# A graph kernel's edge loop: ScalarE takes over the region ends, and the order of its fillers, loads and lower parts is laid out anew

## The reference, cut to what matters

```
x  : 1024 x 512, 16384 edges (src, dst, weight), sorted by dst
A  = zeros(1024, 1024).at[src, dst].add(weight);  deg = sum(A, axis=1)
An = dinv[:, None] * A * dinv[None, :]
h  = x;  for l in 0, 1:  h = leaky_relu((An @ h @ W_gcn[l] + b_gcn[l]) @ W_mlp[l] + b_mlp[l])
x1 = layernorm(x + h)
C  = count of the edges src -> dst, plus self loops;  dis = 1/sqrt(column sums)
h  = relu(dis * C^T (dis * x1 @ W1) + b1);  y = dis * C^T (dis * h @ W2) + b2
out = layernorm(x1 + y)
```

## Time and profile before

| | us |
|---|---|
| median of 3 runs (363.58 to 365.18) | 363.71 |
| the profiled execution | 362.79 |
| its span, first to last instruction | 361.0 |
| TensorE busy | 327.1 (91%) |
| VectorE busy | 191.9 (53%) |
| ScalarE busy | 105.8 (29%) |

### The profile page before, as it was taken

The page is one execution under the profiler, slowest core; times in us unless marked ns, Lnnn a source line. Parts: engine busy times, 40 slices in busy tenths (PEclk is TensorE's granted clock), DMA queues, the critical chain, the costliest instruction groups (busy, mean ns, idle before and its releaser), DMA issues.

```text
span 361.0 us, 5012 instructions
## 1 busy us (share of the span) xinstructions
PE 327.1 (91%) x1976; PEld 266.1 (74%) x1976; DVE 191.9 (53%) x358; ACT 105.8 (29%) x183; POOL 49.4 (14%) x54
## 2 busy tenths in 40 slices
PE   2777998788949989999999999999999999999993
PEld 1555777466737878888888888888888888888882
DVE  6994676963142446103655326767690354323655
ACT  2151336242342344101344201313550355220000
POOL 2000000000010059601000001122184000000111
PEclk9998999999987999999999999999999999999998
DMA  6121003060000000000015000000700000000212
GB/s 228 27 63 58 0 7 114 3 232 4 0 3 0 0 2 0 2 0 0 2 36 196 2 0 0 3 0 2 249 17 0 0 2 0 0 4 3 87 61 87
DMA packets 8592, 13.45 MB, mean 37 GB/s; under 512 B 1906, under 2 KB 2290, under 8 KB 8564
## 3 DMA queue, kind: packets, MB, share of 16 engines
q1 hardware_dynamic: 8564, 13.05, 10.7%
HBM read 10.95 MB, written 2.10 MB: 36 GB/s over the span
## 4 chain that ended last, share of the span: by engine, by line
PE 82%; DVE 12%; issue 3%; ACT 1%; DMA 1%; DVEq 0%; POOLq 0%; POOL 0%; SPq 0%; ACTq 0%
PE psum L568 71%; PE psum L613 5%; DVE hot L912 2%; PE psum L554 2%; PE psum L601 2%; DVE wm_low L984 1%; DVE hot L909 1%; DVE wgt_low L971 1%; DVE sel L907 1%; PE psum L731 1%; DVE adj L966 1%; DMA src_i<-in_src 1%; PE psum L654 1%; PE psum L765 0%; ACT adj L403 0%
## 5 line engine op out<-in xcount | busy, mean ns | idle before, releaser
L613 PEld LDWEIGHTS psum<-hot,sel 128*128 128x128 bf16 x512 | 30.9, 103 | 17.0 <-issue 12.6
L613 PE MATMUL psum<-hot,sel 128*128 128x96 bf16 x512 | 35.6, 218 | 6.2 <-DVE hot L912 3.1
L389 POOL TENSOR_TENSOR small<-small 128x1 f32<-128x1 f32 x16 | 11.9, 742 | 162.4 <-DVE small L1135 162.4
L568 PE MATMUL psum<-at_high,x_high 128*128 128x512 f32 x64 | 26.5, 415 | 1.7 <-DVE x_low L1063 1.7
L568 PE MATMUL psum<-at_high,x_low 128*128 128x512 f32 x64 | 25.6, 401 | 0.0
L568 PE MATMUL psum<-at_low,x_high 128*128 128x512 f32 x64 | 25.6, 400 | 0.0
L971 DVE SCALAR_TENSOR_TENSOR g_low<-psum,g_high 128x512 fp32r<-128x512 f32 x16 | 10.2, 682 | 27.9 <-ACT g_high L403 27.9
L568 PE MATMUL psum<-y_high,at_high 128*128 128x512 f32 x64 | 25.0, 391 | 0.0
L568 PE MATMUL psum<-cnt,x_high 128*128 128x512 f32 x64 | 25.0, 390 | 0.0
L568 PE MATMUL psum<-y_low,at_high 128*128 128x512 f32 x64 | 24.9, 389 | 0.0
L568 PE MATMUL psum<-cnt,x_low 128*128 128x512 f32 x64 | 24.9, 389 | 0.0
(11 more groups left out here) (170 smaller groups left out, 746.6 us busy)
## 6 DMA issues: line engine op xcount, KB each, us to landing
wg_raw<-in_L_gnn_W_gcn SPq DMA_DIRECT2D x2, 1024.0 KB, 5.6
wm_raw<-in_L_gnn_W_mlp SPq DMA_DIRECT2D x2, 1024.0 KB, 6.7
x_raw<-in_x SPq DMA_DIRECT2D x1, 2048.0 KB, 9.1
xs<-in_x SPq DMA_DIRECT2D x1, 2048.0 KB, 9.1
w_raw<-in_L_gnn_W SPq DMA_DIRECT2D x2, 1024.0 KB, 6.9
out<-xs SPq DMA_DIRECT2D x8, 256.0 KB, 2.0
bias_bc<-in_L_gnn_b SPq DMA_DIRECT2D x1, 256.0 KB, 7.4
dst_i<-in_dst SPq DMA_DIRECT2D x1, 64.0 KB, 1.8
```

The source lines that it names most:

```text
L389: pool.tensor_tensor(r[:, 1:2], r[:, 0:1], power[:, 0:1], ALU.pow).then_inc(rstd_ready, 1)
L568: ins = pe.matmul(dest, s, m, start=first and n == 0, stop=end and n == len(pairs) - 1, skip_group_check=True)
L613: ins = pe.matmul(window(c, 1 if k == 0 else 0), stationary, moving, start=False, stop=False, skip_group_check=True)
```

## The change

- **Registers.** The offsets are loaded in 15 loads instead of 10, each after a filler, in two sets of registers in turn.
- **Clears.** Regions 2 to 18 are cleared in the 12 first and 12 last columns of each 64 only (192 columns for 512).
- **Region ends.** ScalarE's `evacuate` waits for the region's last chunk alone. An even region is copied whole; an odd one is copied between its ends, and both its ends (12 columns each, 4 copies in all) go to columns of `adj`/`cnt` five regions ahead, which are not in use yet, or into `late_ends`. VectorE adds them later, for 4, 4, 4, 2, 2 and 3 boundaries at a time (`add_ends`); before region b+5 is copied, ScalarE waits for the add that reads there.
- **Fillers** are placed after chunks, products in two halves; the last product stands after the loop. `adj`'s transposes wait for the adds of their columns, and for `adj_ready` in the general branch only.
- **Orders.** VectorE's queue is written out; the lower parts of Wm come before batch 3, `hw` and the flag after batch 4. The degree matmuls of chunks 0 to 34 come after chunk 34, which waits for the flag and `hw`. The flag also looks at the step between the bases of neighbouring chunks. The second Wm has a buffer of its own (`wm_next`). Batches 0 to 2 share one of the three buffers.

```diff
+    AHEAD = 5
+    LATE_END = NR - 1 - AHEAD
+    BOUNDARIES = [(1, 4), (5, 8), (9, 12), (13, 14), (15, 16), (17, 19)]
+        fillers = {3: [("wgt0", 0, 1)], 7: [("wgt0", 1, 1), ("wgt0", 2, 1)],
+                   15: [("wgt0", 3, 1), ("wc0", 0, 0), ("wc0", 0, 1), ("wc0", 1, 0), ("wc0", 1, 1)],
+                   21: [("wc0", 2, 0)], 27: [("wc0", 2, 1)], 34: [("wc0", 3, 0)], 40: [("wc0", 3, 1)],
+                   47: [("bias0", 0, 1)], 53: [("biasb0", 0, 1), ("wgt1", 0, 1)],
+                   60: [("wgt1", 1, 1), ("wgt1", 2, 1)], 66: [("wgt1", 3, 1)], 73: [("bias1", 0, 1)],
+                   79: [("biasb1", 0, 1), ("wc1", 0, 0)], 86: [("wc1", 0, 1)], 92: [("wc1", 1, 0)],
+                   99: [("wc1", 1, 1)], 105: [("wc1", 2, 0)], 112: [("wc1", 2, 1)],
+                   CH - 1: [("wc1", 3, 0), ("wc1", 3, 1)]}
+        loads = [0, 16, 22, 28, 35, 41, 48, 61, 74, 80, 87, 93, 100, 106, 113]
...
             def evacuate(r):
-                if r:
-                    act.wait_ge(head_added, 2 * r)
-                else:
-                    act.wait_ge(region_done, 1)
+                act.wait_ge(region_done, r + 1)
+                for n, (b0, b1) in enumerate(BOUNDARIES):
+                    if b0 + AHEAD == r:
+                        act.wait_ge(head_added, 2 * (n + 1))
+                lead = WINDOW if r % 2 else 0
                 copy(adj[:, :, d0 + lead:d1], slot[:, 0, :, lead:d1 - d0]).then_inc(evacuated, 1)
                 copy(cnt[:, :, d0 + lead:d1], slot[:, 1, :, lead:d1 - d0]).then_inc(evacuated, 1)
+                if r % 2:
+                    last = min(r + 1, NR - 1)
+                    for kind in range(2):
+                        ends = bass.AP(tensor=psum, offset=(2 * (r % 2) + kind) * BANK,
+                                       ap=[[8 * BANK, P], [PITCH, NB], [REGION, last + 1 - r], [1, WINDOW]])
+                        copy(ends_at(kind, r, last), ends).then_inc(evacuated, 1)
...
             def clear(r):
+                        ends = bass.AP(tensor=psum, offset=(2 * (r % 2) + kind) * BANK,
+                                       ap=[[8 * BANK, P], [PITCH, NB], [PITCH - WINDOW, 2], [1, WINDOW]])
+                        pe.matmul(ends, none[:], zeros[:, 0:2 * COLS].rearrange("p (h a d) -> p h a d", h=NB, a=2),
+                                  start=True, stop=False, skip_group_check=True)
...
+                if c == LATE_HW - 1:
+                    pe.wait_ge(flag_ready, 1)
                     pe.wait_ge(hw_made, 1)
+                    for k in range(LATE_HW):
                         ins = degree(k)
...
+        def ends_at(kind, b0, b1):
+            if b0 > LATE_END:
+                return late_ends[:, kind, :, b0 - LATE_END - 1:b1 - LATE_END, :]
+            return bass.AP(tensor=(cnt if kind else adj), offset=REGION * (b0 + AHEAD) + WINDOW,
+                           ap=[[NB * N, P], [N, NB], [REGION, b1 + 1 - b0], [1, WINDOW]])
...
+            def add_ends(n):
+                b0, b1 = BOUNDARIES[n]
+                dve.wait_ge(evacuated, copies(b1))
                 for kind, sums in enumerate((adj, cnt)):
+                    into = bass.AP(tensor=sums, offset=REGION * b0,
+                                   ap=[[NB * N, P], [N, NB], [REGION, b1 + 1 - b0], [1, WINDOW]])
+                    ends = ends_at(kind, b0, b1)
...
+            make_all(1)
+            make_all(2)
+            for i in range(3):
+                lower_fill("wgt0", i)
+            lower_wm(0)
+            lower_fill("wgt0", 3)
+            make_all(3)
+            check_windows()
+            lower_fill("wc0", 0)
+            make_all(4)
+            lower_fill("wc0", 1)
+            dve.wait_ge(spill_ready, 1)
+            make_hw()
+            take_flag()
+            lower_fill("wc0", 2)
+            make_all(5)
+            add_ends(0)
+            lower_fill("wc0", 3)
+            make_all(6)
+            lower_fill("wgt1", 0)
+            lower_wm(1)
+            add_ends(1)
+            make(7, 0)
+            lower_fill("wgt1", 1)
+            lower_fill("wgt1", 2)
+            for k in range(1, 5):
+                make(7, k)
+            lower_fill("wgt1", 3)
+            make_all(8)
+            add_ends(2)
+            lower_fill("wc1", 0)
+            make_all(9)
+            lower_fill("wc1", 1)
+            uncovered = dve.value_load(flags[0:1, 0:1], min_val=0, max_val=1)
+            add_ends(3)
+            add_ends(4)
+            lower_fill("wc1", 2)
```

More of the change, by code:

```diff
@@ L127, in gnn_resnorm @@
         h3_low = at("h3_low", B1, [P, KD, N], F32R)
+        again(B2, 16 * KB)
+        late_ends = at("late_ends", B2, [P, 2, NB, NR - 1 - LATE_END, WINDOW], F32)
         again(B2)
@@ L445, in upper_fill @@
                     copy(dest[:, i, :], bank(name, i)).then_inc(high_made[name], 1)
[L447 to L453, removed]
+            split_wm(0)
+            for c in stops:
+                if c in closing:
+                    evacuate(closing.index(c))
+                for name, i, part in fillers.get(c, []):
+                    if part:
+                        upper_fill(name, i)
+                if c == 47:
                     split_wm(1)
@@ L621, in degree, with filler @@
                                  start=(c == 0), stop=(c == CH - 1), skip_group_check=True)
-            def filler(name, i):
-                b = claim(name, i)
+            def filler(name, i, part):
+                b = bank(name, i) if name.startswith("wc") and part else claim(name, i)
                 if name.startswith("wgt"):
@@ L671, in _ @@
                 if c in closing:
[L672 to L675, removed]
                     ins.then_inc(region_done, 1)
-                first_batch = BATCHES[0][1]
-                if c == first_batch - 1:
+                if c >= LATE_HW:
+                    ins = degree(c)
+                    if c + 1 in batch_of:
+                        ins.then_inc(batch_used, 1)
+                    if c == CH - 1:
+                        ins.then_inc(loop_done, 1)
+                if c == LATE_HW - 1:
+                    pe.wait_ge(flag_ready, 1)
                     pe.wait_ge(hw_made, 1)
-                    for k in range(first_batch):
+                    for k in range(LATE_HW):
                         ins = degree(k)
-                    pe.wait_ge(spill_ready, 1)
[L683 to L696, removed]
+                        if k + 1 in batch_of:
+                            ins.then_inc(batch_used, 1)
+                for name, i, part in fillers.get(c, []):
+                    filler(name, i, part)
+                if c + 1 in loads:
+                    load_offsets(c + 1)
+                if c == 27:
+                    pe.wait_ge(spill_ready, 1)
+                    b = claim("prep", 4)
+                    pe.transpose(b[0:1, P:2 * P], base, ident[:])
+                    pe.transpose(b[0:1, 0:P], spill, ident[:]).then_inc(prep_done, 1)
+                if c == closing[5]:
+                    uncovered = pe.value_load(flags[0:1, 0:1], min_val=0, max_val=1)
             with pe.If(uncovered > 0):
@@ L983, in lower_wm, with make_all @@
                     dve.wait_ge(wm_high_ready, KD * l + k + 1)
[L984 to L1002, removed]
+                    dve.tensor_tensor(wm_low[:, k, :], (wm_next if l else wm_raw)[:, k, :],
+                                      wm_high[:, k, :].bitcast(F32), ALU.subtract).then_inc(wm_low_ready, 1)
+            def make_all(n):
+                for k in range(5):
+                    make(n, k)
+            make_all(1)
[35 more added lines that the diff above has]
+            lower_fill("wc1", 2)
             def step(ins):
```

142 lines of the change are left out of this document (79 added, 63 removed), and 3 rows, old and new, of the table fillers.

## The result

The changed kernel takes 349.56 us (median of 4 runs, 349.01 to 350.07) against 363.94 before: a ratio of 0.960 (95% interval 0.957 to 0.963), 14.4 us less. The forecast was 344.4, 19.3 less, with a range of 338.5 to 351. Sign and stage were right; the gain is three quarters of what was forecast. In the two profiled executions the span went from 361.0 to 348.1, 12.9 less.

The account below looks back on a forecast made before the run. Only stalls before the first product with A, in and around the edge loop, were taken as winnable. Its start moves from 110.5 to 91.2, saving 19.3: 362.79 becomes 343.5, plus 0.9 gives 344.4 us, range 338.5 to 351.

Parts of the forecast that it names:

- forecast with restarts: First product with A: walk's 89.1 plus 2.1 us for small restarts, 4% of 37 to 89, gives 91.2.
- The gaps at batch starts: TensorE's idle gaps at chunks 16 to 112, behind register loads, would go: 5.7 us in all.
- One of the rivals: Less wait at chunk 34: 2.4 GHz by chunk 8 brings wgt0's last part 1.2 us sooner; 340 us, chance 0.13.
- VectorE from there to the flag: VectorE's queue from 21.5 to the flag at 37.0: builds, spill checks, lower parts, hw, and 1.4 for the flag.
- The wait at chunk 34: TensorE waits 3.1 us for the flag at chunk 34, with 1.9 charged for half clock behind it.
- 0.5 us by the two rows: Price of a register load of 6 or 7 registers, bounds 0.35 and 1.10; load plus 0.6 ends inside its filler.
- loads stick out: Rival: register loads start only when their fillers run out, 12 loads at about 0.9 us; 354 to 355, chance 0.06.
- 4.5 us off TensorE's path: Clears: 17 of 20 shrink by 0.27 us each, taking 4.5 us off TensorE's path.
- the 2.6 us in the list: TensorE's waits for ScalarE at region hand-overs in the kernel before, which the forecast expected to go.
- the 37.5 us of ScalarE's waits: ScalarE's 19 waits for VectorE's boundary add before emptying a region, in the kernel before; expected near nothing afterwards.
- The product after the loop: Last product, 2.81 us of TensorE work, runs under ScalarE's last copies and VectorE's degree steps, formerly idle time for TensorE.
- The clock: Rival: TensorE stays at 1.2 GHz from the wait at chunk 34 on; all of it gives 390 us, chance 0.03.

Follow-up runs that it names:

- the shifted kernel: Kernel before, with its row of offsets kept one element further on, so each of its ten loads starts off a multiple of four: 392.28 us against 363.38, ratio 1.078.
- aligned loads: Changed kernel with each register load rounded out to whole groups of four offsets: 340.37 us against 363.38 for the kernel before, ratio 0.935.
- the fastest version: Changed kernel with loads rounded out to groups of four and first chunks' degree matmuls after chunk 40 instead of 34: 337.57 us against 364.95, ratio 0.928.

## Why the prediction was right or wrong

| point of the walk | forecast | measured |
|---|---|---|
| fourth lower part of wgt0, build of batch 3 starts | 21.5 | 19.9 |
| flag ready, chunk 34 released | 37.0 | 35.4 |
| last product of wc0 ends | 44.4 | 42.5 |
| region 7 out | 51.85 | 50.9 |
| first product of wc1 starts, behind chunk 79 | 63.2 | 65.5 |
| last chunk ends | 83.5 | 91.9 |
| product after the loop ends | 86.4 | 94.8 |
| first product with A (forecast with restarts 91.2) | 89.1 | 97.5 |

By the prediction's own signs it failed in part. It named a first product with A after 97 us as failure (measured 97.5) and allowed no "issue" gap over 0.5 us at batch starts (2.58 and 2.32, behind chunks 60 and 112). The gaps at batch starts, counted as 5.7 us to be won, came back as 5.9. The time stayed inside the range, but outside the 341 to 347 that got 0.62 of the chances.

- **The start** came 1.6 us sooner: TensorE worked at full clock from some 12 us on, not from 20. One of the rivals had this, for 1.2 us.
- **VectorE from there to the flag** took 15.6 us, forecast 15.5. The seven operations of the flag took 1.7 with their waits, for 1.4.
- **The wait at chunk 34** is there, 2.2 us for 3.1, and the half clock behind it, 36.4 to 39.8: right.
- **The register loads are the step that failed**: the overlap was argued for, and its term was put too small. "0.5 us by the two rows" was a line through 0.35 for 4 and 1.10 for 16 registers, for loads "nearly all of 6 or 7 registers". Eleven of 15 are; both large gaps stand at others, of 13 and 15. And both rows were of loads that start at a multiple of four. Nine of the new ones do not; those of 6 or 7 take 1.5 to 1.7 us and those at 61 and 113 take 3.1 and 3.6. In the trace the issue gaps are 5.9 us, and half-clock stretches follow the two longest. The rest of the term holds: a chunk starts 0.7 us after its load ends. Rounding the loads out brings 8.6 us in time and 9.7 at the first product, and moves that product to 87.8, 3.4 before the forecast with restarts and 1.3 before the one without. My rival "loads stick out" had the place but another reason (that the load would start late); it starts early (52.0, before its filler's matmuls at 52.28) and is simply long. Such a load costs 3.80/16 = 238 ns a register in the shifted kernel, one that starts at a multiple of four 1.10/16 = 69 ns. The Trainium skill's figure in "Runtime: NRT & Kernel Launch", "Instruction fetch mechanics", about 200 ns a register, which I set aside for the 69, is near the first; with the second the trace does not agree.
- **Clears.** "4.5 us off TensorE's path" was near as work (0.25 a clear, 17 of them, 4.3 us; 0.18 from a clear's start to the next chunk's, forecast 0.165) and wrong as time: 1.0 (inside the intervals) in the changed kernel, 2.1 to 2.9 with aligned loads.
- **Boundaries.** The adds of 384 elements took 0.55 alone and 0.47 in a row, as forecast, and in the changed kernel no engine waited for them. In the fastest version one does: ScalarE's copy of a region waits 3.2 us for VectorE, and TensorE 0.8 behind it:

```profile
ACT adj L442 <- DVE cnt L1035: 3.2, 1, 3.2
```

So the hand-over is hidden, not gone. What the hand-over had cost was probably undersized: I counted the 2.6 us in the list; taking the adds away, VectorE's work included, gives 5.4 at the first product and 8 to 12 in time. And the 37.5 us of ScalarE's waits, which I put first among the reasons, were mostly waits for the region's chunks.
- **The product after the loop** and the tail: 2.75 us from its end to the first product with A, forecast 2.7 (89.1 - 86.4), at full clock. Right, and the product inside the loop costs 1.8 to 2.3.
- **The clock** did not stay at half level; it fell to it three times, for some 3.4 us each (from 36.4, 57.0 and 87.4), behind gaps of 2.2, 2.58 and 2.32 us, and came back each time. The prediction had charged one such stretch.

So that the forecast came within 5.2 us of the time is in part luck, by errors that cancel: loads and their clock took 9.7 us at the first product; against that stand an earlier start, and the 2.1 us added for restarts, which the aligned kernel hardly needed: its loop runs at full clock after 39 us, and its first product with A starts at 87.8.

## What to carry to other kernels

When a transfer of several items is priced by a line through two rows, ask what the two rows have in common that the new ones won't have: here the address. Look at every "issue" gap by the sequencer's own line; a load of registers that ends last hides behind whatever semaphore wait ends near it. And when a stage is freed of one stall, re-price the others: the short clears were worth 1.0 us, inside the intervals, behind the load gaps and 2 to 3 us without them.

## What the runs showed of the hardware that I had not expected

- A register load from SBUF that starts at an element whose index is a multiple of four (int32) goes by groups of four (4, 8, 12, 16 registers: 0.35, 0.60, 0.85, 1.10 us), with 0.24 us for each left over (6: 0.83 to 0.86, 7: 1.06, 13: 1.11). Started at any other index it takes each register by itself (4: 1.01, 6: 1.48, 7: 1.70, 8: 1.94, 13: 3.11, 15: 3.57, 16: 3.80). Where the row itself begins in SBUF was not varied.
- Loads of 16 registers that are 2.7 us longer, seven of them, and three shorter ones cost the kernel before 28.9 us, more than the 21.6 by which they are longer. Half-clock stretches follow such gaps (0.58 of the clock in the 4 us behind one of 3.2).
